# Edge loop of a graph layer: relu one step earlier, aggregate ahead of reduce, sums with a flag in place of clearing, two in four target comparisons on ScalarE

## The reference

```
h = layernorm(x) @ W.T                      # 8 heads of 32
enc = relu(edge_attr @ edge_W.T + edge_b)   # one row for each edge
alpha = a_src.h[src] + a_dst.h[dst] + sum(enc * h[dst])   # one number for each edge and head
alpha = leaky_relu(alpha, 0.2)
ex = exp(alpha - segment_max(alpha, dst)[dst])
out[n] = sum(ex * h[src]) / sum(ex)         # over the edges whose dst is n
x = x + out + bias
```

## Time and profile before

| | |
|---|---|
| median of 3 runs | 2097.55 us (2096.56 to 2101.39) |
| the profiled execution | 2095.04 us, its span 2093.2 us |
| busy in the span | TensorE 1919.5 us, VectorE 1517.0, ScalarE 1290.6, GpSimd 1206.5 |
| products of the edge loop (L1039) | 440, starts from 104.2 to 1144.7 us |

### The profile page before, as it was taken

One profiled execution on the slowest core, in us unless ns is written; L12 is line 12 of the kernel. 1 busy time (PEld: TensorE's weight loads), 2 busy tenths in 40 slices (PEclk: granted clock), 3 DMA queues, 4 the chain that ended last, 5 costly groups with the idle time before them and its releaser, 6 DMA issues. The chain is left out here.

```text
span 2093.2 us, 45236 instructions
## 1 busy us (share of the span) xinstructions
PE 1919.5 (92%) x12492; PEld 1499.5 (72%) x12492; DVE 1517.0 (72%) x3421; ACT 1290.6 (62%) x3667; POOL 1206.5 (58%) x1137
## 2 busy tenths in 40 slices
PE   7679999999999999999999486899999999999997
PEld 5446666666666666666666245899999999999996
DVE  8769899999999999999999878444444444444442
ACT  4458888888898888888898475233333333333332
POOL 3377777777777776766664000455555555555553
PEclk9879999999999999999999788999999999999998
DMA  9555555555555555555553895222222222222221
GB/s 253 163 153 151 150 157 153 155 153 158 155 155 150 154 151 147 146 144 145 145 141 91 282 331 80 54 36 39 39 36 36 38 40 37 36 36 39 39 37 23
DMA packets 161230, 242.12 MB, mean 116 GB/s; under 512 B 36895, under 2 KB 115519, under 8 KB 160866
## 3 DMA queue, kind: packets, MB, share of 16 engines
q0 software_dynamic: 61920, 139.45, 28.2%
q1 hardware_dynamic: 90362, 92.12, 15.0%
q10 hardware_dynamic: 8712, 7.65, 1.1%
HBM read 202.22 MB, written 36.91 MB: 114 GB/s over the span
## 5 line engine op out<-in xcount | busy, mean ns | idle before, releaser
L750 POOL DMA_INDIRECT arena<-h_tab,src x784 | 757.9, 967 | 285.7 <-issue 195.9
L1774 ACT ACTIVATE arena<-psum,arena 128x128 f32<-128x128 f32 x840 | 239.5, 368 | 519.6 <-PE psum L1724 519.6
L965 PE MATMUL psum<-arena 128*128 128x264 f32 x1760 | 475.3, 394 | 0.7 <-DVE arena L1062 0.6
L1724 PEld LDWEIGHTS psum<-arena 128*128 128x128 f32 x3360 | 393.8, 193 | 7.6 <-issue 2.4
L1724 PE MATMUL psum<-arena 128*128 128x128 f32 x3360 | 394.3, 276 | 2.0 <-DVE arena L1796 2.0
L1740 PE MATMUL psum<-arena 128*128 x1680 | 379.9, 380 | 0.0
L944 PE MATMUL psum<-arena 128*128 128x256 bf16 x2640 | 373.8, 277 | 5.0 <-DVE arena L1039 4.8
L965 PEld LDWEIGHTS psum<-arena 128*128 128x128 f32 x1760 | 300.3, 191 | 82.9 <-issue 46.8
L1686 POOL DMA_INDIRECT out_rows<-arena,src x105 | 212.8, 2027 | 247.6 <-DVE arena L1809 244.6
L1740 PEld LDWEIGHTS psum<-arena 128*128 128x128 f32 x1680 | 311.7, 191 | 37.4
L823 ACT ACTIVATE arena<-iota_row,nrel 128x128 f32<-128x128 f32 x880 | 301.7, 392 | 57.6 <-PE psum L965 57.5
(11 more groups left out here) (242 smaller groups left out, 1921.6 us busy)
## 6 DMA issues: line engine op xcount, KB each, us to landing
arena<-rel_list SPq DMA_DIRECT2D x110, 256.0 KB
arena<-h_tab,src POOLq DMA_INDIRECT x784
arena<-ea_slots SPq DMA_DIRECT2D x440, 27.0 KB
arena<-in_x SPq DMA_DIRECT2D x12, 896.0 KB, 12.6
arena<-in_W SPq DMA_DIRECT2D x16, 512.0 KB, 8.3
arena<-in_W SPq DMA_DIRECT2D x8, 1024.0 KB, 12.3
h_tab<-arena SPq DMA_DIRECT2D x6, 952.0 KB, 9.2
out_rows<-arena SPq DMA_DIRECT2D x5, 896.0 KB, 12.2
```

The source lines that it names most:

```text
L750: pool.indirect_dma_start(rows[:, (p % RING * U + k) * TW:(p % RING * U + k + 1) * TW], None, d.h_tab[:, :], bass.IndirectOffsetOnAxis(ap= ...
L965: last = nc.tensor.matmul(ps[:, AGG + a % 2, 0:HS], oh[:, a % OH, k, :], msg[:, a % MSG, k, :], start=(k == 0), stop=(k == U - 1))
L1724: last = nc.tensor.matmul(ps[:, UP + 2 * b + h // 4, h % 4 * P:(h % 4 + 1) * P], w_now[:, b, m, h * P:(h + 1) * P], xT[:, b, m * P:(m + 1) ...
L1774: last = nc.scalar.activation(hT[:, b, h * P:(h + 1) * P], ps[:, UP + 2 * b + half, h % 4 * P:(h % 4 + 1) * P], ACT.Gelu, bias=b1_now[:, b ...
```

## The change

Six edits, all but one in `edges`:

- relu(g) is called at step 2g - 1 (relu(0) at step 0), ahead of the register loads of step 5 and of one_hot. The buffer of its results has 6 places, where it had 5.
- TensorE does aggregate ahead of reduce at step 1, and loads its registers at the end of step 7.
- clear_ahead goes. take_sums multiplies the accumulator by a flag `keep` (0 for a tile's first slot, else 1) and adds the aggregate, in one instruction. `keep` is made once by VectorE at t = 8 from the tile numbers of the slots, which one more DMA brings to all partitions.
- Of four selects of a chunk, those for g % 4 = 1 and 3 are done by ScalarE at steps 7 and 3: a Square with the partition's number as bias, and a Relu of 1 minus it. TensorE's expand waits on the one or the other.
- ScalarE does the exponent at step 0 ahead of one_hot.
- `oh` and `oht` change places in memory; the second half of W1 of expert 1 is therefore loaded in the attention stage and not at the loop's end.

```diff
-RING, RENC, OH, OT, EB, MSG = 18, 5, 4, 3, 3, 4
+RING, RENC, OH, OT, EB, MSG = 18, 6, 4, 3, 3, 4
-W1_EARLY = (1, 2, 3, 4)
+W1_EARLY = (2, 3, 4)
...
-        by_vector = lambda g: g + 1
+        ON_SCALAR = (1, 3)
+        by_scalar = lambda g: g >= SELECTED and g % 4 in ON_SCALAR
+        scalars = lambda g: sum(by_scalar(n) for n in range(g + 1))
+        by_vector = lambda g: g + 1 - scalars(g)
...
@@ SyncE
             sp.wait_ge(c.links_stored, 32)
+            sp.dma_start(tile_row, d.slots[0:1, 0:SLOTS].partition_broadcast(P)).then_inc(c.links_stored, 16)
             links(0)
...
@@ ScalarE
-                if g >= 8 and g % 4 == 0:
+                if g >= 9 and g % 4 == 1:
                     act.wait_ge(back_done, g // 4 - 1)
...
+            def select(g):
+
+                half, y = divmod(g, 2)
+                act.wait_ge(rel_loaded[half % OT], (half // OT + 1) * 16)
+                part = oht[:, half % OT, 2 * y * UE:2 * (y + 1) * UE]
+                nc.scalar.activation(part, part, ACT.Square, bias=c.iota_p[:, :], scale=-1.0).then_inc(oht_squared, 1)
+                act.wait_ge(oht_squared, 2 * scalars(g) - 1)
+                nc.scalar.activation(part, part, ACT.Relu, bias=c.ones[:, 0:1], scale=-1.0).then_inc(oht_squared, 1)
...
-                if t < SLOTS and t % 2 == 0:
-                    relu(t // 2)
+                if t == 0:
+                    relu(0)
+                if t % 2 and t + 1 < SLOTS:
+                    relu((t + 1) // 2)
...
+                for ch in due(t, 8):
+                    exponent(ch)
                 if 0 <= a + 2 < SLOTS:
                     one_hot(a + 2)
...
+                if t % 2 and t + 3 < SLOTS and by_scalar((t + 3) // 2):
+                    select((t + 3) // 2)
                 for ch in due(t, 7):
                     factor(ch)
                 for ch in due(t, 8):
-                    exponent(ch)
                     node_scale(ch)
-                if t % CS == 0 and 0 < t <= SLOTS:
-                    (j_first,) = load_words(...)
-                if t % 2 and CS < t < SLOTS + CS:
...
-                    clear_ahead(j_first, t % CS // 2)
...
@@ TensorE
-                    if t % CS == CS - 1 and t + 1 < SLOTS:
-                        js = load_words(...)
                 for ch in due(t, 4):
                     to_heads(ch)
                 for ch in due(t, 7):
                     join(ch)
+                if 0 <= a < SLOTS:
+                    aggregate(a)
                 for ch in due(t, 1):
                     reduce(ch)
-                if 0 <= a < SLOTS:
-                    aggregate(a)
+                if t % CS == CS - 1 and t + 1 < SLOTS:
+                    js = load_words(...)
...
@@ VectorE, take_sums
-                if a % CS == 0:
-                    dve.wait_ge(cleared, 1 + CS // 2 * (a // CS + 1))
...
-                nc.vector.tensor_tensor(a_j, a_j, ps[:, AGG + a % 2, 0:HS], ALU.add).then_inc(acc_made, 1)
+                if a == 0:
+                    nc.vector.tensor_copy(a_j, ps[:, AGG, 0:HS]).then_inc(acc_made, 1)
+                else:
+                    nc.vector.scalar_tensor_tensor(a_j, a_j, keep[:, a:a + 1], ps[:, AGG + a % 2, 0:HS], ALU.mult, ALU.add).then_inc(acc_made, 1)
...
+                if t == CS:
+                    dve.wait_ge(c.links_stored, 48)
+                    nc.vector.tensor_tensor(keep[:, 1:SLOTS], tile_row[:, 1:SLOTS], tile_row[:, 0:SLOTS - 1], ALU.is_equal).then_inc(kept, 1)
...
-                if t % CS in AHEAD_OF and SELECTED * 2 <= t + AHEAD_OF[t % CS] < SLOTS:
+                if t % CS in AHEAD_OF and SELECTED * 2 <= t + AHEAD_OF[t % CS] < SLOTS and not by_scalar((t + AHEAD_OF[t % CS]) // 2):
                     select((t + AHEAD_OF[t % CS]) // 2)
...
@@ attention stage, SyncE
-            for e in (0, 5, 6, 7):
+            for e in (0, 1, 5, 6, 7):
                 sp.dma_start(w1[:, 1, e, :], d.W1[e, P:2 * P, :]).then_inc(c.w1_loaded, 16)
```

More of the change, by code:

```diff
@@ L76 @@
 BIG = 1.5e38
-assert GROUPS * GT == J == FIRST[-1] and max(TILES) == GT and SLOTS % CS == 0 and RENC == CS // 2 + 1
+assert GROUPS * GT == J == FIRST[-1] and max(TILES) == GT and SLOTS % CS == 0 and RENC == CS // 2 + 2
 W1_AT = 0
@@ L675, in edges @@
             nc, ctx, "g_relu", "g_square", "g_oh", "g_redtaken", "g_leaky", "g_factor", "g_exp", "g_sources", "g_first")
[L676 to L679, removed]
+        (oht_made, oht_squared, prod_made, msg_made, acc_made, alpha_made, scanned, ends_made, chain_scanned, fall_made,
+         joined, shifted, diag_made, scale_made, rescaled, kept, ends_listed, rows_in, marked, split) = semaphores(
+            nc, ctx, "g_oht", "g_ohsq", "g_prod", "g_msg", "g_acc", "g_alpha", "g_scanned", "g_ends", "g_cscanned", "g_fall",
+            "g_joined", "g_shifted", "g_diag", "g_scale", "g_rescaled", "g_kept", "g_endl", "g_rowsin", "g_marked", "g_split")
         gathered = semaphores(nc, ctx, *[f"g_gat{k}" for k in range(GATS)])
@@ L695, in edges @@
         renc = take(RENC * 2 * 512).rearrange("p (b x e) -> p b x e", b=RENC, x=2)
-        oht = take(OT * 2 * UE).bitcast(BF16).rearrange("p (b e) -> p b e", b=OT)
         ea = c.ea
@@ L700, in edges @@
         msg = take(MSG * U * HS).rearrange("p (b k n) -> p b k n", b=MSG, k=U)
+        tile_row = c.arena[:, at - MSG * U * HS:at - MSG * U * HS + SLOTS].bitcast(I32)
         alpha = take(P)
+        oh = take(OH * UE).rearrange("p (b k n) -> p b k n", b=OH, k=U)
         assert at <= W1_AT + (X + W1_EARLY[0]) * HID
         at, end = REST_AT + EA_WORDS, ARENA
-        oh = take(OH * UE).rearrange("p (b k n) -> p b k n", b=OH, k=U)
+        oht = take(OT * 2 * UE).bitcast(BF16).rearrange("p (b e) -> p b e", b=OT)
         leaky, fwd, top, ex = (take(P) for _ in range(4))
@@ L708, in edges @@
         scale = take(H)
+        keep = take(SLOTS)
         first, others = take(4), take(4)
@@ L827, in one_hot @@
                     nc.scalar.activation(two, two, ACT.Relu, bias=c.ones[:, 0:1], scale=-1.0).then_inc(oh_made, 1)
[L829 to L834, removed]
             def first_edge(ch):
@@ L935, in expand @@
                 if x == 0:
-                    pe.wait_ge(oht_made, by_vector(s // 2))
+                    if by_scalar(s // 2):
+                        pe.wait_ge(oht_squared, 2 * scalars(s // 2))
+                    else:
+                        pe.wait_ge(oht_made, by_vector(s // 2))
                     if s == 5 * CS:
@@ L1002, in _ @@
                     expand(t, js)
-                    if t % CS == CS - 1 and t + 1 < SLOTS:
-                        js = load_words(nc, c.slots[0:1, t + 1:t + 1 + CS], mybir.EngineType.PE, 0, J - 1)
                 for ch in due(t, 4):
@@ L1008, in _ @@
                     join(ch)
+                if 0 <= a < SLOTS:
+                    aggregate(a)
                 for ch in due(t, 1):
                     reduce(ch)
-                if 0 <= a < SLOTS:
-                    aggregate(a)
+                if t % CS == CS - 1 and t + 1 < SLOTS:
+                    js = load_words(nc, c.slots[0:1, t + 1:t + 1 + CS], mybir.EngineType.PE, 0, J - 1)
                 for ch in due(t, 2):
@@ L1041, in message @@
             def message(a):
+                if a == 0:
+                    dve.wait_ge(kept, 1)
                 if a % CS == 0:
@@ L1058, in take_sums @@
                     dve.wait_ge(acc_made, a)
+                if a == 1:
+                    dve.wait_ge(kept, 1)
                 if a % CS == 0 and a:
```

6 lines of the change are left out of this document (removed).

## The result

The changed kernel takes 2153.4 us (median of 4 runs, 2150.52 to 2153.98), the kernel before 2099.22 on the same chip (4 runs, 2096.56 to 2101.39): ratio 1.0265, 95% interval [1.0252, 1.0278]. Slower by 54 us; 2144 was forecast, with a range of 2110 to 2168. In the profiled executions the spans are 2151.8 and 2093.2 us, at the same mean clock of TensorE (0.968).

What follows compares the result with a forecast made beforehand. A ring from reduce through ScalarE's list, exponent, to_rows and expand was taken to bound the loop; 46.9 turns x 1.0 = +47 us, +1.4 (W1), -0.5 (tail), 0 to +3 early, gave 2144 us, range 2110 to 2168.

Steps and rivals of the forecast that it cites:

- The ring of relu and encode: Edge loop: early relu waits for the previous step's encode, aggregate for ScalarE; turn 19.71 against 18.65 us; chance 0.72.
- +1.0 a turn: Edge loop: growth taken for each eight-step turn, from +1.06 less part of the change-over into reduce; 46.9 turns give +47 us.
- The register loads: ScalarE, step 5: loads could hide wholly behind the earlier relu, -1.08 us; if not hidden, +0.45 a turn.
- The 0.15 that the aggregate might cover in front of reduce: TensorE, to_rows to reduce: the aggregate now in between may cover part of the 0.98 us change-over, to 0.15 less.
- The flag: VectorE's sums: multiplying by the flag adds 0.06 us to each, +0.48 us of VectorE a turn; bounds 0 to 0.1.
- The comparison: Two of four move from VectorE (-0.52 us a turn) to ScalarE, 1.40 us each, 2.80 a turn; bounds 1.07 to 1.54.
- W1: Attention stage: expert 1's 0.5 MB load ahead of the x rows lengthens VectorE's wait by 1.4 us; range 0 to 2.2.
- The tail: Loop's end: loses a wait for reduce of about 1 us, pays 0.06 on some 16 sums; -0.5 us.
- The first eight turns, 0 to +3: First 160 us of the loop: the gathers' 20.3 us a turn covers the new ring's 19.7; 0 to +3 us.
- The loop is a ring: Kernel before, edge loop: reduce, ScalarE's list of work, exponent, to_rows, expand, reduce make the whole turn, 18.65 us.
- -0.66 with cheap comparisons: Lower bound on the new ring's growth if ScalarE's comparisons cost less: 0.66 us off, leaving +0.4 a turn.
- VectorE decides: Edge loop, rival: relu's waits cost nothing and VectorE's list sets the turn, 18.08 us; 2084 us, faster; chance 0.07.

Runs made afterwards that it cites:

- the faster version: Kernel before, no flag or moved comparisons: relu at steps 1, 4, 6, 7, reduce behind step 2's expand, exponent before one_hot, later register load; 2090.68 us, ratio 0.9977.

## Why the prediction was right

**The ring of relu and encode** was the likeliest case and is what happened: relu waits 1.10 us at step 3 and 0.67 at step 7, aggregate 0.76 at step 6, and ten links add up to 19.87 against 19.71. Encode ahead of aggregate and three relu put back show it as the cause: some 34 and 43 of 54 us come back without a change of the work done. That all four put back bring only 10 shows a second ring nearly as long behind it (19.65 against 19.86), from aggregate ahead of reduce over sums and the relu of step 2; the prediction didn't have that one.

**Mis-sized terms.** +1.0 a turn became +1.12. Of the ring's 0.16, 0.17 is exponent to to_rows (0.52, not 0.35): factors (L996) wait for the exponent's neighbour L870 and stand ahead of to_rows. The register loads are covered but for 0.19 (relu to squares 1.09, not 0.90), some of which a comparison at 1.37 instead of 1.40 gives back. The mean turn lies 0.05 above the one that I followed. In the paced part this makes 52.5 instead of 47. The 0.15 that the aggregate might cover in front of reduce was covered only by 0.03 (1.84 against 1.87).

**The flag** costs what was forecast, +0.06 us each:

```profile
L1074 DVE SCALAR_TENSOR_TENSOR arena<-arena,psum 128x264 f32 x161 | 77.2, 480 | 2.7
```

480 ns against 423. **The comparison** at 1.37 is the forecast's 1.40. **W1** was put down at 1.4: the attention stage grew by 1.3, VectorE's wait for x by 1.4.

**The tail** is the term with the wrong sign: +2.7, where -0.5 was put down. It "loses a wait for reduce", I wrote; the opposite holds. Sums in the last turn, in the timeline of the changed kernel and then of the one before:

```profile
1203.29 0.59 ACT L853 COPY arena<-psum 128x512 f32<-128x512 f32 x1 [3.77 <-PE psum L962]
```

```profile
1147.44 0.59 ACT L845 COPY arena<-psum 128x512 f32<-128x512 f32 x1 [0.37 <-PE psum L955]
```

They start 6.0 us after the last product, before 2.8. Two things make this up. Reduce stands behind an aggregate that waits for VectorE's take_sums, so it starts 2.7 us after the product and not 0.8. And it takes longer itself: reduce in the changed kernel, then before, and all engines of the changed kernel around it:

```profile
1200.02 3.19 PE L962 MATMUL psum<-arena,block_ones 128*32 128x512 f32 x16
```

```profile
1145.45 1.93 PE L955 MATMUL psum<-arena,block_ones 128*32 128x512 f32 x16 [0.23 <-DVE arena L1039]
```

```profile
1199.50:1202.50 3.00, 3.00 (x14) 0.59 (x16) 2.02 (x4) 0.02 (x1) 0.00 (x0) 0.50 0.00 0
```

The granted clock was 0.50, the lower level (1.2 GHz), in these 3 us, and 1.00 in the same place of the kernel before. TensorE had stood still for 0.7 and 0.8 us just before. The changed kernel with the comparisons on VectorE has the same order and the same two pauses, but its clock stayed at 1.00, its reduce took 1.92, and its tail is 1.1 us longer than that of the kernel before. So about 1.1 of the 2.7 is the order and 1.6 the clock.

**Routing** (+1.3) and **the experts** (+0.6) had no term. Nothing in them was changed, and in the fourteen traces routing takes between 50.6 us (the kernel before) and 52.0, the experts between 771.3 and 773.1: both differences are no larger than this scatter. The first eight turns, 0 to +3 in the sum, came out within +0.2.

**A reading that was off.** Of ScalarE's stop of 1.08 us in the earlier trace rows the prediction says that the aggregate asked for is "two steps old". It is that of the step before: it starts at 929.92 and takes 1.06, so it was done 0.5 us ahead of the square. The register loads still end last, and nothing in the sum changes.

**What the prediction read too simply.** "The loop is a ring" of ScalarE's list: the flag alone shows that a second one, VectorE's list with its wait for aggregate, was level with it. The sum came out since the new ring is longer than both. But the single prices in it can't be had one by one: aggregate first costs 1.44%, relu early 1.64%, the flag 0.64%, 3.7% together, and the whole change 2.65%; the comparisons fill 2.75 us of the ring and are worth 0.19 of it. The range's lower bound, "-0.66 with cheap comparisons", was worked out by that wrong rule.

**The rival "VectorE decides"** comes near in another order: once sums, relu and encode no longer wait for each other, VectorE hardly waits any more, and the turn is 18.5; the 18.08 that the rival gave was seen nowhere.

The Trainium skill, Perfetto Trace Analysis, "Optimizing Scalar/DVE Operations", says that it may make sense to move work from a saturated DVE to Scalar. In this order the runs do not bear it out: with the two comparisons back on VectorE the ratio falls from 1.0265 to 1.0219. In the order of the faster version, where VectorE is busy for 97%, no run shows it.

## What to carry to other kernels

When engines work fixed lists and release one another by semaphores, find the rings: add up starts to starts from an instruction to its next turn, across engines, before and after the change; the longest sets the pace, and a wait for another engine's newest result is what lengthens it. An instruction is called early only if its input is also made early: move producer and consumer together. What a shortened link gives back is bounded by the lead over the next ring, so measure an edit in the order in which it is to live, and don't add up edits measured alone.

## What was not expected of the hardware

One chip ran the kernel before in 2529.86 us where the others took 2097, with single instructions of VectorE as long as elsewhere (the product 737 ns on both), but gaps of up to 8 us marked "remote" (the profile doesn't show what ended them) and a mean granted clock of TensorE of 0.90 instead of 0.968. Why that chip stood still stays open. On it an edit worth 1.4% elsewhere shows a ratio of 1.0000: a ratio to runs on the same chip doesn't help where something else sets the pace.

The granted clock fell to 0.50 for 3.4 us at the loop's end in some traces (the changed kernel, aggregate first, both with relu put back) and not in others with the same order (the comparisons back on VectorE). In the changed kernel's tail it makes up 1.6 us of the growth, the order 1.1. What decides whether it falls there stays open.
